# Keys of 41 chunks turned by VectorE in 32x32 blocks and device memory instead of by TensorE

## What is computed

```python
def attention(x):                       # x: layer-normalized input
    q, k = relu(heads(x @ Wq)) + 0.001, relu(heads(x @ Wk)) + 0.001
    v = heads(x @ Wv)
    context = cumsum(einsum('bhnd,bhne->bhnde', k, v), axis=2)
    D_inv = 1.0 / einsum('bhnd,bhnd->bhn', cumsum(k, axis=2), q)
    attn = einsum('bhnd,bhnde,bhn->bhne', q, context, D_inv)
    return merge(attn) @ Wo + bo

def ffn(x):                             # x: layer-normalized input
    h = silu(fp4_linear(x, w_gate)) * fp4_linear(x, w_up)
    return fp4_linear(h, w_down)        # fp4_linear rounds both operands

x = x + attention(layernorm(x))
x = x + ffn(layernorm(x))
```

## Time and profile before

| | before |
|---|---|
| median of the runs | 1523.23 us |
| the profiled execution, its own time | 1523.17 us |
| its span | 1521.2 us |
| TensorE busy | 1492.5 us |
| VectorE busy | 1117.6 us |
| ScalarE busy | 652.4 us |
| GpSimd busy | 722.7 us |
| DMA, mean over the span | 88 GB/s |
| granted TensorE clock | 0.997 |

### The profile page before, as it was taken

How to read it: one execution, slowest core, us unless ns; L and a number is a source line. 1 busy time by engine, 2 the same in 40 slices (tenths; PEclk the granted TensorE clock), 3 DMA queues, 4 the chain that set the end, 5 groups by cost and what they waited for, 6 DMA issues and landing times.

```text
span 1521.2 us, 55070 instructions
## 1 busy us (share of the span) xinstructions
PE 1492.5 (98%) x23652; PEld 1401.8 (92%) x23652; DVE 1117.6 (73%) x2322; ACT 652.4 (43%) x1165; POOL 722.7 (48%) x822
## 2 busy tenths in 40 slices
PE   9889999999999999999999999999999999999998
PEld 7878999999999999999999999999999999999998
DVE  8786767776777777778677777776778677777767
ACT  5434444343443444443343443444444343443433
POOL 4313555444554545554544554535554544554543
PEclk9999999999999999999999999999999999999999
DMA  5101333233233233233232233332333233233210
GB/s 168 34 2 44 88 99 108 73 102 95 74 113 91 90 102 95 76 112 92 81 111 81 89 112 92 87 99 83 92 113 95 76 112 87 83 112 92 82 51 14
DMA packets 159360, 133.25 MB, mean 88 GB/s; under 512 B 12944, under 2 KB 150672, under 8 KB 159120
## 3 DMA queue, kind: packets, MB, share of 16 engines
q1 hardware_dynamic: 159120, 129.75, 28.9%
HBM read 68.09 MB, written 61.60 MB: 85 GB/s over the span
## 4 chain that ended last, share of the span: by engine, by line
PE 80%; DVE 4%; DMA 3%; issue 2%; SPq 2%; POOL 1%; ACT 1%; DVEq 0%; POOLq 0%; ACTq 0%
PE bank L607 61%; PE bank L740 3%; PE bank L729 3%; PE bank L774 3%; PE bank L691 3%; PE bank L808 3%; DMA hq_away<-hq_blocks 1%; DMA attn_away<-probs 1%; PE bank L835 1%; PE bank L855 1%; PE bank L617 1%; PE bank L886 1%; SPq L546 1%; PE bank L713 1%; DMA attn<-attn_away 1%
## 5 line engine op out<-in xcount | busy, mean ns | idle before, releaser
L607 PE MATMUL bank<-xT_hi,wqk_hi 128*128 128x256 f32 x1024 | 211.6, 288 | 3.3 <-ACT qkT L1127 2.0
L607 PE MATMUL bank<-xT_hi,wqk_lo 128*128 128x256 f32 x1024 | 204.0, 280 | 0.0
L607 PE MATMUL bank<-xT_lo,wqk_hi 128*128 128x256 f32 x1024 | 203.7, 280 | 0.0
L1127 ACT ACTIVATE qkT<-bank 128x512 f32<-128x512 f32 x256 | 149.3, 595 | 111.3 <-PE bank L607 109.0
L1517 POOL TENSOR_TENSOR attnT_lo<-attn,attnT_hi 128x1024 fp32r<-128x1024 f32 x58 | 156.9, 2706 | 68.2 <-ACT attnT_hi L1200 68.2
L1577 POOL TENSOR_SCALAR qkT<-qkT 128x512 f32<-128x512 f32 x256 | 159.4, 635 | 61.4 <-ACT qkT L1127 60.1
L607 PEld LDWEIGHTS bank<-xT_hi,wqk_hi 128*128 128x128 f32 x1024 | 157.5, 189 | 7.8 <-issue 4.3
L1556 POOL TENSOR_TENSOR xq<-x_scaled,x_scale 128x256 f32<-128x256 f32 x64 | 49.4, 772 | 228.6 <-DVE x_scaled L1743 228.6
L607 PEld LDWEIGHTS bank<-xT_hi,wqk_lo 128*128 128x128 f32 x1024 | 156.9, 189 | 0.0
L607 PEld LDWEIGHTS bank<-xT_lo,wqk_hi 128*128 128x128 f32 x1024 | 156.9, 189 | 0.0
L1250 ACT ACTIVATE silu<-bank 128x352 f32<-128x352 f32 x128 | 58.7, 458 | 218.6 <-PE bank L607 206.9
(11 more groups left out here) (218 smaller groups left out, 3812.1 us busy)
## 6 DMA issues: line engine op xcount, KB each, us to landing
attn<-attn_away SPq DMA_DIRECT2D x232, 128.0 KB, 2.9
hq_away<-hq_blocks SPq DMA_DIRECT2D x58, 384.0 KB, 3.1
hq<-hq_away SPq DMA_DIRECT2D x232, 96.0 KB, 2.3
attn_away<-probs SPq DMA_DIRECT2D x58, 256.0 KB, 2.7
attn_away<-probs SPq DMA_DIRECT2D x116, 128.0 KB, 2.7
x_in<-in_L_attn_x SPq DMA_DIRECT2D x32, 256.0 KB, 2.9
out<-out_sb SPq DMA_DIRECT2D x64, 128.0 KB, 2.7
qkT<-in_L_attn_Wq SPq DMA_DIRECT2D x1, 1024.0 KB, 8.5
```

The source lines that it names most:

```text
L607: at = pe.matmul(dst, lhs_at(kt), rhs_at(kt), start=first and kt == 0, stop=last and kt == k_tiles - 1)
L1127: act.activation(flat(qkT[:, 2 * m:2 * m + 2, :]), bank[bank_of["qk", unit_place(u, 1), n]][:], ACT.Relu).then_inc(qk_relu, 1)
```

## The change

For 41 chunks, those of positions 0 to 2 from chunk 8 to chunk 61 (`SENT_KEYS`), TensorE's eight transposes and ScalarE's two copies are left out. In their place VectorE transposes the keys of the chunk in 32x32 blocks into a new tile key_stage (`block_keys`), SP sends the tile to device memory in one transfer and fetches it back to the same tile in four, with the blocks in their places, and ScalarE copies it to k_tok in one instruction. The keys of chunk g + 1 are turned in step g, so the key tiles of a half are now projected first (`KEYS_FIRST`) and the scores wait for six tiles instead of four. In SP's order the keys' send and fetch each stand ahead of the attention's, in odd steps and in the first step of a sequence. In even steps ScalarE's copy of the keys stands ahead of its copy of the attention. To make room, x gets three tiles in place of four: the bias is added in place, the result is written over x2 and stored from there.

```diff
+    SENT_KEYS = [g for g in range(2 * CHUNKS, END) if g % CHUNKS < CHUNKS - 1]
+    EARLY_K_UNITS = range(SENT_KEYS[0] // HALF, END // HALF)
...
-        x_in = [sb(f"x_in{k}", [P, HALF, DIM]) for k in range(2)]
-        x_bias = [sb(f"x_bias{k}", [P, HALF, DIM]) for k in range(2)]
+        x_bufs = [sb(f"x_in{k}", [P, HALF, DIM]) for k in range(3)]
+        key_stage = sb("key_stage", [P, INNER])
...
+        KEYS_FIRST = [4, 5, 6, 7, 0, 2, 1, 3]
+
         def qk_tile(u, n):
-            return (QK_ORDER if u else FIRST_QK_ORDER)[n]
+            return (KEYS_FIRST if u in EARLY_K_UNITS else QK_ORDER if u else FIRST_QK_ORDER)[n]
+
+        def half_of_qk(u):
+
+            return PAIRS * u + (6 if u in EARLY_K_UNITS else 4)
...
             def load_x(u, h):
 
-                if u >= 2:
-                    sp.wait_ge(xn_ready, u - 1)
-                    sp.wait_ge(x_bias_ready, u - 1)
-                sp.dma_start(x_in[h][:], x_halves[u]).then_inc(x_loaded[h], 16)
+                if u >= len(x_bufs):
+                    sp.wait_ge(x2_ready, HALF * (u - len(x_bufs) + 1))
+                sp.dma_start(x_of(u)[:], x_halves[u]).then_inc(x_loaded[h], 16)
...
+            def send_keys(n):
+                sp.wait_ge(key_blocks_ready, sent_keys(n) + 1)
+                if sent_keys(n):
+                    sp.wait_ge(keys_back, 16 * GROUPS * sent_keys(n))
+                sp.dma_start(keys_away, key_stage[:]).then_inc(keys_sent, 16)
+
+            def fetch_keys(n):
+                sp.wait_ge(keys_sent, 16 * (sent_keys(n) + 1))
+                at = keys_away.rearrange("(a r) (j e) -> j r a e", r=GROUP, j=GROUPS)
+                to = key_stage[:].rearrange("p (a e) -> p a e", a=GROUPS)
+                for j in range(GROUPS):
+                    sp.dma_start(to[GROUP * j:GROUP * (j + 1)], at[j]).then_inc(keys_back, 16)
...
                     if exists(g - 4, END - 4):
                         store(g - 4)
+                    if c == 0 and g + 1 in SENT_KEYS:
+                        send_keys(g + 1)
                     if g in SENT_ATTN:
                         send_attn(g)
+                    if c == 0 and g + 1 in SENT_KEYS:
+                        fetch_keys(g + 1)
+                    if g in SENT_ATTN:
                         fetch_attn(g)
...
+                    if g + 1 in SENT_KEYS:
+                        send_keys(g + 1)
                     if g in SENT_ATTN:
                         send_attn(g)
+                    if g + 1 in SENT_KEYS:
+                        fetch_keys(g + 1)
+                    if g in SENT_ATTN:
                         fetch_attn(g)
...
             def scores(b, c, g, u):
                 t = c % 2
-                pe.wait_ge(qk_ready, PAIRS * u + 4)
+                pe.wait_ge(qk_ready, half_of_qk(u))
...
                     scores(b, c, g, u)
-                    turn_k(b, c, g)
+                    if g not in SENT_KEYS:
+                        turn_k(b, c, g)
...
+            def staged_keys_to_tokens(b, c):
+                act.wait_ge(keys_back, 16 * GROUPS * (sent_keys(CHUNKS * b + c) + 1))
+                act.wait_ge(kv_early_done, (CHUNKS - 1) * b + c)
+                act.wait_ge(kv_done, (CHUNKS - 1) * b + c)
+                act.activation(k_tok[:].rearrange("p (n a e) -> p n a e", n=PAIRS, a=GROUPS), staged_keys, ACT.Copy
+                               ).then_inc(k_ready, 2)
...
             def even_step(b, c):
                 g, u = CHUNKS * b + c, UNITS * b + c // 2
                 high_x(c, u + 1)
+                if g in SENT_KEYS:
+                    keys_by_tokens(b, c)
                 if g - 1 in SENT_ATTN:
                     high_sent_attn(g - 1)
                 if g > WARM:
                     square_h(g - 3)
-                for n in range(2):
-                    keys_to_tokens(b, c, n)
+                if g not in SENT_KEYS:
+                    keys_by_tokens(b, c)
...
                 high_sent_hq(g - 4)
-                if c == 1:
+                if u + 1 in EARLY_K_UNITS:
+                    if sent_keys(g + 1):
+                        act.wait_ge(key_blocks_ready, sent_keys(g + 1))
+                elif c == 1:
                     act.wait_ge(av_done, 2 * (g + 1))
...
+            def block_keys(n):
+                t, u = n % HALF, n // HALF
+                dve.wait_ge(qk_ready, PAIRS * u + PAIRS // 2)
+                if n != SENT_KEYS[0]:
+                    before = SENT_KEYS[sent_keys(n) - 1]
+                    dve.wait_ge(k_ready, 2 * ((CHUNKS - 1) * (before // CHUNKS) + before % CHUNKS + 1))
+                dve.transpose(key_blocks, qkT[:, PAIRS:2 * PAIRS, t * P:(t + 1) * P].rearrange(
+                    "p n (j c) -> p n j c", c=GROUP)).then_inc(key_blocks_ready, 1)
...
+                if CHUNKS <= g < LAST:
+                    dve.wait_ge(out_stored[(g + 1) % 2], 16 * (g // 2 - 1))
...
-                dve.tensor_tensor(out_sb[:, (g + 1) % 2, :], bank[bank_of["down", place(g + 3), 0]][:, 0:DIM],
+                dve.tensor_tensor(x2_of(g), bank[bank_of["down", place(g + 3), 0]][:, 0:DIM],
                                   x2_of(g), ALU.add).then_inc(out_ready, 1)
...
                 add_early(g)
+                if c == 0 and g + 1 in SENT_KEYS:
+                    block_keys(g + 1)
...
                 residual(g - 4)
+                if g + 1 in SENT_KEYS:
+                    block_keys(g + 1)
```

More of the change, by code:

```diff
@@ L459, in build_program, with sent_keys, turned_keys @@
         attn_blocks = probs[:, 0:INNER].rearrange("p (a o e) -> p a o e", a=GROUPS, o=2)
+        def sent_keys(n):
+            return len([g for g in SENT_KEYS if g < n])
+        def turned_keys(n):
+            return (CHUNKS - 1) * (n // CHUNKS) + n % CHUNKS - sent_keys(n)
+        key_blocks = key_stage[:].rearrange("p (j n e) -> p n j e", j=GROUPS, e=GROUP)
+        staged_keys = key_stage[:].rearrange("p (a n e) -> p n a e", a=GROUPS, e=GROUP)
         def by_raw_attn(t):
@@ L726, in turn_k @@
                 for n in range(2):
-                    k = banks.take(pe, ("k", place(g), n), b, k_ready, lambda b, n=n: 2 * ((CHUNKS - 1) * b + c) + n + 1)
+                    k = banks.take(pe, ("k", place(g), n), b, k_ready, lambda b, n=n: 2 * turned_keys(CHUNKS * b + c) + n + 1)
                     for j in range(4):
@@ L1186, in keys_to_tokens, with keys_by_tokens @@
                 g = CHUNKS * b + c
-                act.wait_ge(k_turned, 2 * ((CHUNKS - 1) * b + c) + n + 1)
+                act.wait_ge(k_turned, 2 * turned_keys(g) + n + 1)
                 act.activation(k_tok[:, n * 512:(n + 1) * 512], flat(turn[bank_of["k", place(g), n]][:]),
                                ACT.Copy).then_inc(k_ready, 1)
+            def staged_keys_to_tokens(b, c):
[4 more added lines that the diff above has]
+                               ).then_inc(k_ready, 2)
+            def keys_by_tokens(b, c):
+                if CHUNKS * b + c in SENT_KEYS:
+                    staged_keys_to_tokens(b, c)
+                else:
+                    for n in range(2):
+                        keys_to_tokens(b, c, n)
             def high_attn(n, half):
```

27 lines of the change are left out of this document (14 added, 13 removed).

## The result

The changed kernel takes 1553.57 us (median of 4 runs, 1551.02 to 1556.93), the kernel before in the same session 1523.77: a ratio of 1.0201, 95% interval 1.0185 to 1.0218. It is 2% slower; the prediction said 1499.4 and 1484 to 1520.

The account below looks back on a forecast made before the run. TensorE, busy 1492.5 of 1521.2 us, was taken as the bound. 1523.2 - 37.0 (transposes removed) + 11.2 (first chunks' waits) + 2.0 (second chunks' waits) = 1499.4 us, range 1484 to 1520.

Parts of the forecast that it names:

- TensorE as the bound, 37.0 us to gain: On TensorE, 41 chunks lose eight key transposes each, at 0.93 or 0.85 us a chunk: 37.0 us saved.
- The attention comes back later through SP's order: In odd steps the keys' send and fetch precede the attention's fetch: attention 1.4 us later, bounds 1.1 and 2.7.
- The chain behind L1200 is 1.07 us shorter, 4.88: First chunks, ScalarE's attention copy (L1200) to TensorE's L808: 4.88 us for 5.95, the keys' copy now standing ahead.
- 0.60 + 4.88 - 4.68 = 0.80 us of wait: First chunks: attention's copy start plus chain, less TensorE's arrival, counted from T: 0.80 us of wait each, 11.2 in all.
- In the third chunk ... just in time: nothing: Third chunks: attention's copy waits behind the keys' copy, state's sum ends at 824.6, TensorE wants it at 824.70: no cost.
- Second chunks, 0.15 us of wait: Second chunks: TensorE waits for k_tok, keys' fetch standing behind the attention's send: 0.15 us each, 2 us in all.
- The slower one named crowded transfers: Rival on DMA: keys' and attention's landings 1.3 us late, first and second chunks wait, 1535 us; chance 0.15.
- The waiting scores: Rival in odd steps: VectorE's 1.25 us delays the last add_eps, TensorE waits about 0.6 us in 27 steps, 1515; chance 0.12.
- A store a step ahead, x in three buffers: nothing: Buffers of x: three tiles, bias added in place, result written over x2 and stored a step ahead: no cost.

Follow-up runs that it names:

- e14: e12 with one eighth of the keys' bytes in as many transfers, the rest of the keys left over from the blocks; 1497.17 us, ratio 0.9843.
- e1: e0 with VectorE's block transposes of the keys back in, still without any transfer of keys; 1508.79 us, ratio 0.9901.
- e2: The change with one eighth of the keys' bytes in as many transfers, the send cut down likewise; 1527.37 us, ratio 1.0027.
- e3: The change with GpSimd's rounding of the attention in even steps held (the gate) until VectorE's rounding of h is done; 1558.07 us, ratio 1.0233.
- e4: The change with ScalarE, in even steps, copying the attention and squaring h ahead of copying the keys; SP's order unchanged; 1547.45 us, ratio 1.0187.
- e0: The change without VectorE's block transposes and all transfers of the keys, ScalarE copying a tile of zeros to k_tok; 1504.61 us, ratio 0.9869.
- e13: e12 with TensorE turning the keys of second chunks again, so only first and third chunks send keys; 1511.39 us, ratio 0.9938.
- e16: The change with SP's odd-step order alone made send attention, send keys, fetch attention, fetch keys; ScalarE's order unchanged; 1604.71 us, ratio 1.0548.
- e12: The change with attention ahead of keys in SP's odd-step queue, and ScalarE's even-step keys' copy behind those of attention and xq; 1513.76 us, ratio 0.9947.
- e15: e13 with GpSimd's rounding of the attention in even steps waiting until VectorE's roundings are made; 1518.24 us, ratio 0.9975.

## Why the prediction was wrong

By steps, the 54 us between forecast and measurement are 29 in the 14 first chunks (16.72 us for 14.77 - 0.93 + 0.80 = 14.64), 15 in the 13 third ones (15.76 for 14.61) and 10 in the 14 second ones (31.17 for 30.49).

**TensorE as the bound, 37.0 us to gain.** Right in kind, but the 37.0 never came whole: with the attention back as early as before and few bytes on the way the kernel takes 1497 (e14), 24 us less than before by the ratio.

**The attention comes back later through SP's order.** Right in kind, too small: forecast T+0.60, measured T+1.24. The 1.4 us had 1.1 to 2.7 as bounds, and 2.05 came out. In the mean of the 14 timelines of SP's queue the attention's fetch is issued 1.41 us later than before (T-4.03 for T-5.44), so the place in the queue was sized right. What the sum had at nothing is the rest: issuing takes 1.85 us for 1.76, and the copy starts 3.42 us behind the last issue for 2.87, 0.55 more. For that stretch the forecast had 2.7, from one chunk. The attention landed after 3.4 us in the median (2.9 before). From e1 over e2 to the change, A moves by 0.93 with the nearly empty transfers and by 0.97 more with their bytes, which I had priced only in the send (3.4 us for 3.1).

**"The chain behind L1200 is 1.07 us shorter, 4.88".** This is the step that failed, and the largest one. The sum is right as far as ScalarE goes: 4.86 is what e3 measures with the gate. But I had followed the chain over ScalarE and VectorE and not looked at what GpSimd does beside them. The later attention puts GpSimd's rounding of 2.4 us on top of VectorE's first rounding, which grows from 0.88 to 1.96 us and takes the 1.07 back: 5.93 in the mean. It could have been read from the kernel before: the two roundings of the same size in its first chunk, in VectorE's timeline, differ there already, and over all steps L1741's mean was 1.23 us.

```profile
868.17 1.01 DVE L1741 SCALAR_TENSOR_TENSOR h_scaled<-h_square,h_scaled 128x704 f32<-128x704 bf16 x1
869.22 0.89 DVE L1743 SCALAR_TENSOR_TENSOR h_scaled<-h_square,h_scaled 128x704 f32<-128x704 bf16 x1
```

The Trainium skill, page "SBUF — State Buffer", section "SBUF: two separate sides", says that VectorE with two SBUF inputs and GpSimd share a port pair that one instruction holds for its whole length. The trace agrees: L1804 at 1.97 us ends 0.75 us after GpSimd's rounding, nearly its whole length of 0.88. In all 27 first and third chunks of the change it ends 0.74 to 0.76 us after GpSimd's. In e4, where it starts 2.1 us behind GpSimd's start for 1.2, it ends as long after it and takes 1.0 us in first chunks.

First chunks in one line: the forecast was 0.60 + 4.88 - 4.68 = 0.80 us of wait, measured 1.24 + 5.93 - 5.18 = 1.99. Of the missing 1.19, 0.64 is the attention, 1.05 the chain, and TensorE's own later arrival takes 0.50 off the wait but not off the time. L853 thus starts 1.69 us behind its forecast, and these steps are 2.08 us longer than forecast; the 0.4 us between the two lie behind L853, where five of the six falls of the clock lie that are told of below.

**"In the third chunk ... just in time: nothing".** Failed by the same term: the 4.83 us to the end of the state's sum, 4.88 to TensorE, became 5.99 to TensorE, and TensorE waited 0.79 in the mean, in e0 already 0.71, where no key is moved.

**Second chunks, 0.15 us of wait.** Too small. The 0.85 us that the removal saves there were lost entirely (31.19 to 31.17; e0 has 30.44, e2 30.70). In their steps TensorE waits 2.5 us before L785, where keys were late, and 5.2 before L853 and L652, nearly all in three gaps of 1.6 to 1.7 us without a named releaser; e13 shows that leaving these chunks to TensorE costs nothing.

**The clock was not in the sum.** TensorE's row of windows (busy, granted clock, DMA share, GB/s) at the wait of 1.96 us that ended at 980.22:

```profile
978.00:982.00 4.00, 2.04 (x56) 0.83 0.01 4
982.00:986.00 4.00, 4.00 (x26) 0.74 0.44 167
986.00:990.00 4.00, 4.00 (x74) 1.00 0.79 209
```

A clock between the two levels, 1.2 and 2.4 GHz, means part of the window at the lower one: (0.17 + 0.26) x 4 = 1.7 us lost. Over windows of 4 us from 190 to 1478 there are six such places in the change, 10.2 us in all, each behind a wait of 1.7 to 2.1 us; one in the kernel before (1.7 us), none in e13 and e14. Not every such wait has one: nine of the 14 first chunks of the change wait 1.7 to 2.1 us without it, and chunk 22 waits 3.5 without it.

**The rivals.** The slower one named crowded transfers, gave 1535 and had 0.15: its side was right, and the bytes are over half of it (26 us of 45 from e1 to the change). Its price was not: it had landings late by 1.3 us, and the attention's was late by 0.55. What it lacked is the port and the clock. The waiting scores did not come: L736 waits once for add_eps, 0.5 us, and e1 puts all of VectorE's added work at 4 us. "A store a step ahead, x in three buffers: nothing" held as far as TensorE's waits show; no run isolates it.

TensorE arrives 0.50 us later than forecast in first chunks of the change, 0.18 in e14 and 0.23 in e0. Of the 0.50, 0.16 are seven waits before L819 that end 0.1 us behind VectorE's xqT_lo, as in e16. Not settled: the rest of it, and what the gaps without a releaser before L853 are (7.5 us in the change, 4.8 in e14). No run isolates them.

## What to carry to other kernels

When a tensor's way is changed, list everything that shares its queue and everything that is late by a fixed margin; the tensor with the least spare goes first, in the DMA queue and in the engine that takes the results in, and both orders change together. A chain of waits is timed over all engines that work beside it: shifting one operation by 2 us can put two on the same port. A gain of 37 us on the bounding engine was worth 19 us with nothing in its place, 8 with transfers in the right order (e12), and became a loss of 30 in the wrong one.

## What the runs showed that I had not expected

- VectorE's rounding of 128x704 with two SBUF inputs takes 0.88 us alone and 1.96 when GpSimd's 128x1024 subtraction started 1.2 us ahead of it; GpSimd's takes 2.38 in the mean then, and as long with the rounding out of its way (e3).
- A landing order that contradicts an engine's own order is worse than a slow transfer: 1604.7 us with the attention first in the queue and second on ScalarE, against 1523.5 with both first, 31 of the 81 us being time at the lower clock.
- Holding GpSimd back to free the port did free it in e3 and e15 and did not pay: its input tile attn is written again soon after, and VectorE then waits for GpSimd (0.79 us in the rows of e3) instead.
- The best kernels are e12 and e13, 0.5 and 0.6% faster than before; a lighter way for the keys' bytes would be worth up to 17 us more, an estimate from e12 and e14.
